# Layer-1 attention on one core: another order of the local rounds' side work, grouped projections, six probability buffers in the local rounds

## The reference, cut to what matters

```
x = x + global_latent_attn(rmsnorm(x))   # k, v = (x @ kv_down) @ k_up, v_up; causal
x = x + local_gqa_attn(rmsnorm(x))       # k, v = x @ wk, x @ wv; causal, 32 keys back
# each: q, k = rope, then RMS norm by head; softmax(q k / sqrt(8)) v, then @ wo
```

## Time and profile before

| | |
|---|---|
| median of 3 runs | 2310.27 us (2308.59 to 2312.89) |
| the profiled execution's own time | 2308.52 us |
| its span in the profile | 2306.8 us |
| PE busy | 2147.4 us, 93% |
| DVE, ACT, POOL busy | 1449.5, 1210.5, 1046.8 us |
| layer-1 attention | from about 1477 to 2101 us of the span: 40 us of prologue, four global rounds of about 91 us, four local ones |

### The profile page before, as it was taken

How to read it: one execution, slowest core, us unless ns; L and a number is a source line. 1 busy time by engine, 2 the same in 40 slices (tenths; PEclk the granted TensorE clock), 3 DMA queues, 4 the chain that set the end, 5 groups by cost and what they waited for, 6 DMA issues and landing times. The chain is left out here.

```text
span 2306.8 us, 41147 instructions
## 1 busy us (share of the span) xinstructions
PE 2147.4 (93%) x15812; PEld 1410.1 (61%) x15812; DVE 1449.5 (63%) x3302; ACT 1210.5 (52%) x1796; POOL 1046.8 (45%) x982
## 2 busy tenths in 40 slices
PE   6999999999999999998999999879999998888997
PEld 4555565555655565557888888634444445556777
DVE  5787757776687757773666566546555454567633
ACT  4555535554455535553333333267786876665653
POOL 2777757777577747784323232423332321110001
PEclk9999999999999999999999999889999999999999
DMA  2000000000000000021000000000000000003001
GB/s 78 1 1 1 1 1 1 1 1 1 1 1 1 2 1 1 1 47 31 1 1 1 1 1 1 1 1 1 1 1 1 1 1 1 2 8 75 1 1 37
DMA packets 36197, 18.17 MB, mean 8 GB/s; under 512 B 16666, under 2 KB 33828, under 8 KB 36004
## 3 DMA queue, kind: packets, MB, share of 16 engines
q1 hardware_dynamic: 36004, 15.54, 2.7%
HBM read 13.44 MB, written 2.10 MB: 7 GB/s over the span
## 5 line engine op out<-in xcount | busy, mean ns | idle before, releaser
L318 POOL TENSOR_TENSOR a_first<-a_first,a_ring 128x512 f32<-128x512 f32 (+3 forms) x352 | 558.0, 1585 | 253.7 <-PE a_o_ps L542 216.7
L1963 ACT ACTIVATE g_probsT<-g_s_ps 128x1024 f32<-128x1024 f32 (+2 forms) x448 | 369.0, 869 | 136.9 <-PE g_s_ps L1832 82.7
L676 ACT ACTIVATE a_ring<-a_st 128x768 f32<-128x768 f32 (+1 forms) x256 | 228.5, 918 | 86.0 <-PE a_st L527 84.3
L773 DVE TENSOR_REDUCE a_part_max<-a_mx 128x2 f32<-128x1024 f32 x128 | 156.5, 1223 | 131.7 <-PE a_mx L490 130.5
L796 DVE RECIPROCAL a_row_inv<-a_row_inv 128x256 f32<-128x256 f32 x128 | 218.6, 1732 | 24.0 <-ACT a_row_inv L664 24.0
L542 PE MATMUL a_o_ps<-a_ring,a_v 128*64 128x512 f32 (+3 forms) x1280 | 226.4, 474 | 1.6 <-POOL a_ring L300 1.4
L1243 ACT ACTIVATE m_silu<-m_up,m_b 128x512 f32<-128x512 f32 x160 | 109.8, 689 | 219.6 <-PE m_up L1178 218.1
L1863 PE MATMUL g_o_ps<-g_probsT,g_values 128*32 128x512 f32 (+5 forms) x2688 | 206.7, 419 | 5.2 <-POOL g_probsT L1708 5.1
L1708 POOL TENSOR_SCALAR_AFFINE_SELECT g_probsT<-g_probsT 128x512 f32<-128x512 f32 x128 | 88.4, 693 | 244.9 <-ACT g_probsT L1963 244.7
L1832 PE MATMUL g_s_ps<-g_qT,g_kT 64*128 64x512 f32 (+3 forms) x896 | 173.7, 435 | 27.4 <-ACT g_probsT L1963 21.7
L490 PE MATMUL a_mx<-a_k_hi,a_q_hi 64*128 64x512 f32 (+3 forms) x768 | 146.9, 404 | 24.6 <-DVE a_largest L780 17.1
(11 more groups left out here) (344 smaller groups left out, 4271.1 us busy)
## 6 DMA issues: line engine op xcount, KB each, us to landing
m_w<-in_L_ffn_rw SPq DMA_DIRECT2D x2, 1024.0 KB, 8.9
s_w<-in_L_ffn_w SPq DMA_DIRECT2D x1, 2048.0 KB, 8.8
s_w<-in_L_ffn_w SPq DMA_DIRECT2D x4, 512.0 KB, 9.6
out_x<-x SPq DMA_DIRECT2D x8, 256.0 KB, 2.3
m_w<-in_L_ffn_rw SPq DMA_DIRECT2D x2, 512.0 KB, 6.5
x<-in_L_attn_x SPq DMA_DIRECT2D x2, 256.0 KB, 3.1
a_outT<-in_L_attn_w_k SPq DMA_DIRECT2D x1, 512.0 KB, 5.3
a_outT<-in_L_attn_w_q SPq DMA_DIRECT2D x1, 512.0 KB, 6.1
```

The costliest lines, as they stand in the source:

```text
L318: pool.tensor_tensor(total[:, h, q:q + w], total[:, h, q:q + w], probs_of(n, u)[:, h, off:off + w], ALU.add).then_inc(added, 1)
L676: act.activation(probs_of(n, u)[:, :, 0:w], st_ps[u % 2][:, :, 0:w], ACT.Exp).then_inc(exp_done, 1)
L773: last = dve.tensor_reduce(part_max[:, i, :], mx_ps[:], AX.X, ALU.max)
L1963: act.activation(out, src.rearrange("p k (j n) -> p k j n", j=at_once), ACT.Exp, scale=float(HD) ** -0.5).then_inc(exp_done, 1)
```

## The change

Four things, all in `layer1_attention`:

1. In local rounds the side work has another order: both `project` uses stand at steps 8 and 10 (were 10 and 12), `att` at 12 (was 8). On DVE `rotate`, `square_heads`, `sum_heads` stand two steps earlier (11, 12, 13); the guess and two Newton steps come at 15 and the third at 16; `scale_heads` stays at 17; `fill_slots` go to 23, 24, 25, 27, 29. On POOL the rotation goes to 11 and its sum to 14. On ACT `high_parts` go to 22, 23, 24, 26, 28.
2. A global projection does half a sequence (two banks, four blocks) at once: four blocks against `w_in`, then four against `w_up`, in place of one after the other in each block.
3. `local_pair` puts `fill_banks` in front of the values of the pair before.
4. In local rounds a step uses one half of a `probsT` buffer, so that there are six; the exponent of step s waits for the values of step s - 6.

```diff
+LOCAL_FROM = BATCH * STEPS
+LOCAL_COLS = SEQ // 2
+def probs_col(r, n):
+    return (r * STEPS + n) // 3 % 2 * LOCAL_COLS if is_local(r) else 0
...
-                     (8, "att", old, 0), (10, "project", new, 0), (12, "project", new, 1), (14, "back", own, 0),
+                     (8, "project", new, 0), (10, "project", new, 1), (12, "att", old, 0), (14, "back", own, 0),
...
-                        if x < ROUNDS and n == (13 if is_local(r) else 15):
+                        if x < ROUNDS and n == (11 if is_local(r) else 15):
                             rotate(x)
-                        if x < ROUNDS and n == (16 if is_local(r) else 18):
+                        if x < ROUNDS and n == (14 if is_local(r) else 18):
                             add_rotation(x)
...
+                def project_global(k, x, half):
+                    x_read(pe, "input", x, 0, half)
+                    for two in range(2):
+                        bank_free(k + two)
+                        for out, rows in projected(k + two, 2 * half + two):
                             pe.matmul(out[:, 0:D], normedT[:, rows], w_in[0][:, 0:D], start=True, stop=True)
+                    x_read(pe, "latent", x, 0, half)
+                    for two in range(2):
+                        for out, rows in projected(k + two, 2 * half + two):
                             last = pe.matmul(out[:, D:], latT[:, rows], w_up[:], start=True, stop=True)
+                        last.then_inc(x_filled, 1)
...
                     mask_scores(r, n)
                     mask_scores(r, n + 1)
+                    fill_banks(r, n)
                     late_r, late_n = (r, n - 2) if n else (r - 1, STEPS - 2)
                     if is_local(late_r):
                         weigh_all(late_r, late_n)
                         weigh_all(late_r, late_n + 1)
                     else:
                         weigh_last_of(late_r, late_n)
-                    fill_banks(r, n)
-                    fill_banks(r, n + 1)
...
                         if step >= 3 and unit == 0:
-                            act.wait_ge(pv_done, step - 2)
-                        col = a - kb * P if is_local(r) else a
+                            act.wait_ge(pv_done, step - 5 if step >= LOCAL_FROM + 3 else step - 2)
+                        col = a - kb * P + probs_col(r, n) if is_local(r) else a
...
-                HIGHS = {18: 0, 19: 1, 20: 2, 21: 3, 22: 4}
+                FIRST_HIGHS = {18: 0, 19: 1, 20: 2, 21: 3, 22: 4}
+                LOCAL_HIGHS = {22: 0, 23: 1, 24: 2, 26: 3, 28: 4}
...
-                            if n == (13 if local else 15):
+                            if n == (11 if local else 15):
                                 rotate(x, 0)
                                 rotate(x, 1)
-                            if n == (14 if local else 16):
+                            if n == (12 if local else 16):
                                 square_heads()
-                            if n == (15 if local else 17):
+                            if n == (13 if local else 17):
                                 sum_heads()
-                            if n == (16 if local else 18):
-                                inverse_roots(x)
+                            if n == (15 if local else 18):
+                                guess_roots(x)
+                                better_roots(2 if local else 3)
+                            if local and n == 16:
+                                better_roots(1)
                             if n == (17 if local else 19):
                                 scale_heads(x)
-                            for i in ({19: (0,), 20: (1,), 21: (2,), 22: (3,), 23: (4,)} if local else
+                            for i in ({23: (0,), 24: (1,), 25: (2,), 27: (3,), 29: (4,)} if local else
```

More of the change, by code:

```diff
@@ L1764, in project_latent, with projected, project_local @@
                               stop=True).then_inc(x_filled, 1)
-                def project(k, x, quarter):
+                def projected(k, quarter):
+                    return [(x_ps[k % 2][:, i * 256:i * 256 + 192], slice((quarter * 2 + i) * P, (quarter * 2 + i + 1) * P))
+                            for i in range(2)]
+                def project_local(k, x, quarter):
                     x_read(pe, "input", x, 0, quarter // 2)
[L1768 to L1776, removed]
+                    for out, rows in projected(k, quarter):
+                        last = pe.matmul(out, normedT[:, rows], w_in[1][:], start=True, stop=True)
+                    last.then_inc(x_filled, 1)
[4 more added lines that the diff above has]
+                        for out, rows in projected(k + two, 2 * half + two):
                             pe.matmul(out[:, 0:D], normedT[:, rows], w_in[0][:, 0:D], start=True, stop=True)
+                    x_read(pe, "latent", x, 0, half)
+                    for two in range(2):
+                        for out, rows in projected(k + two, 2 * half + two):
                             last = pe.matmul(out[:, D:], latT[:, rows], w_up[:], start=True, stop=True)
-                    last.then_inc(x_filled, 1)
+                        last.then_inc(x_filled, 1)
                 def turn_back(k, x, h, half):
@@ L1797, in fill_banks @@
                 def fill_banks(r, n):
-                    for k in uses_at(r, n):
+                    for k in uses_at(r, n) + uses_at(r, n + 1):
                         _, _, what, x, i, half = USES[k]
+                        if what == "project" and not is_local(x):
+                            if half == 0:
+                                project_global(k, x, i)
+                            continue
                         bank_free(k)
@@ L1807, in fill_banks @@
                         elif what == "project":
-                            project(k, x, 2 * i + half)
+                            project_local(k, x, 2 * i + half)
                         elif what == "back":
@@ L1903, in local_pair @@
                         weigh_last_of(late_r, late_n)
-                    fill_banks(r, n)
-                    fill_banks(r, n + 1)
-                for n in range(STEPS):
+                for n in range(0, STEPS, 2):
                     fill_banks(-1, n)
@@ L1980, in _ @@
                                 read_bank(k)
-                        if not 0 <= r < BATCH and r + 1 < ROUNDS and n in HIGHS:
-                            high_parts(r + 1, HIGHS[n])
+                        highs = FIRST_HIGHS if r < 0 else LOCAL_HIGHS
+                        if not 0 <= r < BATCH and r + 1 < ROUNDS and n in highs:
+                            high_parts(r + 1, highs[n])
             @block.vector
@@ L2063, in sum_heads, with guess_roots, better_roots @@
                     own.did(dve.tensor_tensor(t_even, parts[0], parts[1], ALU.subtract))
-                def inverse_roots(x):
+                def guess_roots(x):
                     dve.wait_ge(qk_var, x + 1)
                     own.did(dve.tensor_scalar(rs[:].bitcast(I32), ssq[:].bitcast(I32), -0.5, ROOT_GUESS, ALU.mult, ALU.add))
-                    for _ in range(3):
+                def better_roots(times):
+                    for _ in range(times):
                         own.settle()
```

## The result

The changed kernel takes 2284.95 us (median of 4 runs, 2283.78 to 2285.43), the kernel before 2309.43 us beside it (4 runs, 2305.52 to 2312.89): 0.9899 of it, 95% interval 0.9884 to 0.9915, 24.5 us less. The forecast was 2291.3, its own range 2286 to 2297: the result lies 1 us beyond the fast end of it, and more was gained than the sum said. The profiled execution has a span of 2283.7 us, 23.1 less than before.

What follows compares the result with a forecast made beforehand. PE was taken to set the pace in global rounds, waits on DVE and ACT to hold up local ones; 6.0 + 1.9 + 11.4 − 0.3 = 19.0 us saved gives 2289.5 profiled, 2291.3 as median, range 2286 to 2297.

Steps and rivals of the forecast that it cites:

- ACT's wait at the high parts: Local rounds: ACT's 5.60 us wait for scale_heads, which held up pair 20's exponents, would be gone.
- The stall of pair 4: Local rounds: PE would wait 2.3 us for DVE's late bank read, before 0.7, a loss of 1.7 us.
- rival A: Local rounds: half clock after pair 4, or ACT slipping further from pair 22, leaves 9 us gained, 2301; chance 20%.
- rival C: Local rounds: half clock behind pairs 4 and 16 costs 20.4 us against 19.0 gained, 2312; chance 4%.
- the layout by hand: Round 5 worked out in its new order: 52.9 us instead of 56.7, 3.8 saved, three times, 11.4.
- pairs 22 to 30: End of a local round: ACT is the bound, without a gap from 39 to 53 us; last read ends at 52.9.
- The length of a pair: Local rounds: with side work in front of the values an undisturbed pair stays 2.80 us long.
- Six buffers: Local rounds: the removed wait was already counted; a loss of 0.3 us in the first local pair.
- Grouping: Global projections, rounds 0 to 2: 1.0 us saved in each of six pairs, 6.0 us, between 0 and 6.8.
- rival E: Rounds 0 and 2: the granted clock's dips go too, 4 us more gained, 2287 or less; chance 4%.
- rival D: No change: one half-clock stretch a local round and no gain from grouping, 2307.5; chance 6%.
- The prologue: Grouped projections before the rounds, most at the half clock: 1.9 us saved, between 0.5 and 2.6.

Runs made afterwards that it cites:

- order_only: Kernel before with part 1 alone, the new local order of side work on all engines: 2293.2 us, ratio 0.9929.
- scale_behind_read: Changed kernel with DVE's scaling of the next input moved behind the second read of the old back in local rounds: 2270.9 us, ratio 0.9847.
- order_group: Kernel before with only parts 1 and 2, the new local order and grouped projections: 2277.7 us, ratio 0.9875.
- fill_six_only: Kernel before with only parts 3 and 4, side work in front of values and six buffers: 2310.5 us, ratio 1.0002.
- six_only: Kernel before with part 4 alone, six probability buffers in local rounds: 2307.7 us, ratio 0.9992.
- no_six: Changed kernel with part 4 undone, so three buffers with side work still in front of values: 2312.5 us, ratio 1.0012.

## Why the prediction was right, and where its sizes were off

*The time.* The forecast was 19.0 us of gain, measured are 24.5 by medians and 23.1 by the spans. 2286, the fast end of the range, was missed by 1 us. The upper bounds that the prediction gives for its terms (6.8, 2.6 and three times 5.8, less 0.3) reach 2284, and it does not say how 2286 came of them. That the total came out near is in part luck: 3.0 us lie in code that wasn't changed, and round 7 gave 2.3 that were not booked, against 2.3 too few in rounds 4 to 6.

*ACT's wait at the high parts.* Right, and it is part 1's alone: order_only took it away and brought 17.5 us in rounds 4 to 6.

*The stall of pair 4.* Place and size right (2.34 us). The prediction booked it as a loss of 1.7 us a round and gave the fall of the clock behind it as rival A. That rival's mechanism came along with the forecast: the half clock stood behind pair 4 in all three rounds, and in rounds 4 and 6 in pair 16 too, which is the place of rival C. Both rivals priced a stretch at up to 3.4 us; measured it cost 1.4 to 1.5, for example 9.8 us for pairs 4 and 6 of round 5 where 8.2 would stand without it. The five stretches cost 7 us together. By this estimate rounds 4 to 6 would have gained 16 us without them, so the layout by hand was 5 us too slow elsewhere: in the length of a pair (below), and in pairs 22 to 30, booked at 16.1 us with ACT without a gap and measured at 14.75 in round 5. The 8.8 us against 11.1 are the sum of these two errors of opposite sign. scale_behind_read shows the late read and what follows it to cost 14 us, and order_group that parts 3 and 4, put in to help, cost 7. The sentence "the old fall came after 4.4 idle us of 5.1, this is 2.5 of 3", meant as an argument against, was none.

*The length of a pair.* The sum said that with part 3 "the pair stays 2.80 long". That step failed: 2.70, and 2.64 in pair 0. Mask and transposes have the same tile shape (0.56 from one to the other, before 0.64 from mask to values), so one change of shape less stands in a pair. It is also the term behind round 7, booked at 0, measured −2.3: fill_six_only has −2.4 there, six_only −0.8, so about 1.6 us are part 3's and 0.8 part 4's.

*Six buffers.* Booked at nothing, nearly right by themselves (six_only has 0.8 us in round 7), with a loss of 0.3 us in the first local pair that did not come (4.47 us, before 4.62). But the prediction did not say that part 3 rests on them, which no_six shows.

*Grouping.* 6.0 us in rounds 0 to 2 forecast, 6.2 measured over rounds 0 to 3. The size is right for a pair: at equal clock a round shrinks from 91.1 to 89.1 us, 1.0 a pair, as booked. That the sum agrees is luck: round 1 grew by 1.2 us, with a clock of 0.96 where it had been 1.00, and round 2 lost 6.4, from 0.95 to 1.00, of which grouping has 2.0. The other 4.4 are what rival E foresaw, and 2284.95 lies in its "2287 or less": round 2 is at the full clock in eight of the nine kernels with grouping by half a sequence and in none of the five others. Round 1, with two new stretches at the half clock, took 3.2 of it back. In rival D grouping gives nothing and yet the 1.9 us of the prologue, which are grouping's too, stay in the sum; without them D is 2309.4. The Trainium skill (TensorE: Matmul & The Clock Gate, Part 3, "The mechanism") has the rule on loads of like row groups; it did not decide here: grouped records pass at 0.13 us.

*The prologue.* 2.9 instead of 1.9: the term mis-sized is the clock. The second half was booked at the half level, with 0.23 us a record, and ran at the full one (8 records in 1.13 us, granted clock 1.00). Before, the first half had run at the full level too (1484.77 to 1487.88) and only the second at 0.50, so "most at the half clock" was a misreading:

```profile
1484.73 1.13 PE L1789 MATMUL g_x_ps<-g_w_in,g_normedT 128*128 128x128 f32 x8 [0.35 <-ACT g_values L1959]
...
1487.58 0.82 DVE L2072 TENSOR_TENSOR g_part<-g_qk,g_cos 128x640 f32<-128x640 f32 x1 [12.84 <-ACT g_values L1959]
```

*Ahead of the attention.* 3.0 us of the span's 23.1 lie in code that is the same in both. Over all thirteen profiles besides the one before, the attention began between 1473.5 and 1479.5, with no relation to the edits that I could find. The cause isn't shown. The 6 us between these profiles bound what one profile can tell.

## What to carry to other kernels

Where one engine reads the banks that another fills, put each such read ahead of the reader's own long chain: the same instructions in another order were worth 21 us here, nearly as much as the whole change. A part that is a loss in one order can be a gain in another (side work in front of the values cost 5 us by medians, then gained 4.6), so try it again after the stall beside it is gone. When work is moved in front of an operation, list everyone who waits for that operation: here DVE's keep, and ACT's exponents, which needed the other buffers.

## What the runs showed of the hardware

A change of tile shape on PE, with the change of operand that goes with it, costs 0.165 us between full-float32 products of 128 by 128 and 32 by 128 (3.11, 2.45 and 2.12 us with 7, 3 and 1 of them).

In the changed kernel and the experiments with its wait in pair 4, the granted clock fell with a wait of 2.3 us in pair 4 each time; in round 5 this made pair 6 1.5 us longer (4.13 us, in scale_behind_read 2.62). The length of the wait alone does not decide. Behind 1.90 us in pair 16 it fell in rounds 4 and 6 of the changed kernel and not in its round 5, nor behind 1.91 in scale_behind_read or 1.58 in order_only; behind 1.56 us in pair 4 of round 5 of no_six it fell. What else decides, no run here shows.
